# The row maxima of an attention stage turned by VectorE in 32x32 blocks instead of by TensorE, sent in 128-byte pieces, and SyncE's sends in another order

## Chip, core and metric

One core of a Trainium2 chip. The metric is the device time in microseconds of the whole program, as the median of its runs.

## What is computed

For an input x of 8 x 1024 x 256 the result is x + attention(LN(x)) + experts(LN(x)). The attention has 16 heads of 16 channels and an ALiBi bias:

```python
kqv = x @ W_kqv.T
k_, q_, v_ = jnp.split(kqv, 3, axis=-1)
...
bias = alibi_slopes(H)[:, None, None] * rel.astype(jnp.float32)
score = jnp.einsum('bhsd,bhnd->bhsn', q, k) / scale + bias[None]
attn = jax.nn.softmax(score, axis=-1)
out = jnp.einsum('bhsn,bhnd->bhsd', attn, v)
```

The other part is a mixture of 8 experts (top 2) with a shared expert, in its own stages of the kernel, which the change does not touch.

## The kernel before

The program has three stages: `front` (layer norm, projections, routing, shared expert), `experts`, and `attend`, which the change is in. `attend` works on 32 groups of 4 heads of one batch (GROUPS, GH). For each group keys, queries and values lie in one of three sets of buffers, `k_op`, `q_op` and `v_op`. A softmax needs the row maxima before the exponentials, so every score is made twice. The first time (L1405, `max_half`) it lies with queries on the partitions, in the two PSUM buffers `p1`, and VectorE reduces it to `part` (L1255, `max_unit`, 1024 columns at a time); after 8 such units `join` (L1263) puts the smaller of the two negated halves into 8 columns of `neg`. The second time (L1418, `score`) keys lie on the partitions, in the three PSUM buffers `p2`, and the negated maximum of each query comes in as row 50 (or 114 for the second head of a pair) of `q_op`, beside a row of ones in `k_op`. ScalarE takes the exponential into `probs` (L1379), and TensorE multiplies that with the values into `p_o` (L1430, `products`). Every half group of 512 queries is copied to `o_sb` (L1367, `output_copy`), turned (L1442) and copied to `o_t` (L1357).

The two are offset by a group: while the scores of group g are made, the maxima of group g + 1 are made beside them, a score on one half of the array's rows and a maxima matmul on the other. A group has 64 units n of scores (HALF = 32 of them per half) and 32 units w of maxima (MAX_UNITS). TensorE's loop over n writes score n, maxima half n, and after each odd n one side of the products of 4 units ago. It begins a PSUM buffer of `p2` when `s2_read` tells that ScalarE has read it, and one of `p1` when `s1_read` tells that VectorE's reduction of two units before is done.

To get from `neg` (queries on partitions) to a row of `q_op`, TensorE transposes the 16 columns of a half's `neg` (L1411, `turn_max`) into a `p2` buffer: for the second half of the own group at n = 5 (OWN_TURN), and for the first half of the next group at n = 37 (TURN_AT). ScalarE copies it to `m_row`, 16 rows of 128 (L1348, `row_copy`). SyncE (SP) then sends it with 4 DMAs (L1144, `send_max`), each of which writes 4 pieces of 512 B into one row of `q_op`. The scores of a half wait for these DMAs (`m_in`) at the half's first unit. `use2` counts the uses of `p2`, the turns among them.

SP's program in a group is written out in `group` under `block.sync`: first the wait for the products of the group before (`pv_done`) and the 15 DMAs that load group g + 2 (L171, L175, L177, `load`), then `send_max` of the own second half, then `send_max` of the next group's first half. SP issues in this order. VectorE's program in a group is 32 reductions, 4 joins (each one unit late, but the last one right after the last unit) and up to two reciprocals (L1271, `invert`). Before group 0 stands a prologue of 32 maxima units without scores.

Of the kernel before, what the change touches and what calls it, by code (L numbers as in the profile page):

```python
# [1055 lines left out]
def attend(nc, keep, scratch, out):  # L1056
    with ExitStack() as ctx:
# [9 lines left out]
        neg = [sb(f"neg{i}", [P, 8 * PAIRS], F32R) for i in range(2)]  # L1067
        m_row = [sb(f"m_row{i}", [8 * PAIRS, P], F32R) for i in range(2)]
# [13 lines left out]
        names = ("passed ones_in init s1_ps s1_read neg_ok s2_ps s2_read pv_done pv_side o_ok rec_ok "  # L1082
# [11 lines left out]
        TURN_AT = HALF + 5  # L1094
        OWN_TURN = 5
# [3 lines left out]
        K_LOAD = 14  # L1099

        def ring1(g):
            return (g + 1) * R1

        def turns_at(g):

            out = [OWN_TURN] + [h * HALF + OUT_TURN for h in range(2) if g or h]
            return sorted(out + ([TURN_AT] if g < GROUPS - 1 else []))

        def use2(g, n):

            before = 1 + sum(UNITS + len(turns_at(i)) for i in range(g))
            return before + n + sum(t < n for t in turns_at(g))
# [16 lines left out]
        def _(sp):  # L1129
# [20 lines left out]
            send_max(0, 0, 0, 0)  # L1150
# [94 lines left out]
        def _(dve):  # L1245
            v = nc.vector

            dve.sem_inc(s["s1_read"], 2)

# [8 lines left out]
            def join(c_, done):  # L1258
# [4 lines left out]
                v.tensor_tensor(neg[half][:, 8 * pair:8 * pair + 8], pt[:, 0].rearrange("p x q -> p (x q)"),  # L1263
                                pt[:, 1].rearrange("p x q -> p (x q)"), ALU.min).then_inc(s["neg_ok"], 1)
# [39 lines left out]
            for w in range(MAX_UNITS):  # L1304
                max_unit(w, w)
                if w % CHUNK == CHUNK - 1:
                    join(w // CHUNK, w + 3)

            def group(g, u, turn, has_prev, has_next):
                due = None  # L1310
                for w in range(MAX_UNITS):
                    if has_next:
                        max_unit(ring1(g) + w, w)
                        if due is not None:
                            join(*due)
                            due = None
                        if w % CHUNK == CHUNK - 1:
                            due = (w // CHUNK, ring1(g) + (w + 3))
                    for half in range(2):
# [17 lines left out]
        def _(act):  # L1337
# [31 lines left out]
            row_copy(0, 0, 0)  # L1369

            def group(g, u, turn, has_prev, has_next):
                for n in range(UNITS):
# [7 lines left out]
                    if n == OWN_TURN:  # L1380
                        row_copy(g, use + 1, 1)
                    elif n == TURN_AT and has_next:
                        row_copy(g + 1, use + 1, 0)
                    elif n % HALF == OUT_TURN and (half or has_prev):
# [10 lines left out]
        def _(pe):  # L1395
# [11 lines left out]

            def turn_max(g, half, use):
                pe.wait_ge(s["neg_ok"], g * CHUNKS + PAIRS * (half + 1))
# [125 lines left out]
```

## Time and profile before

| | |
|---|---|
| median of the runs | 2465.36 us (3 runs, 2455.23 to 2470.11) |
| span of the profiled execution | 2465.2 us |
| the profiled execution's own time | the page gives the span alone |
| TensorE (PE) busy | 2399.8 us, 97% |
| VectorE (DVE) busy | 1899.4 us, 77% |
| ScalarE (ACT) busy | 1561.3 us, 63% |
| GpSimd (POOL) busy | 782.9 us, 32% |
| mean granted TensorE clock | 0.982 of full speed |

PE is a TensorE matmul, PEld its weight load, SPq the issue of a DMA on SyncE's queue. Times in a timeline are microseconds from the span's start. "x8" behind a row means that eight instructions in a row were merged into it; the second number is the time from the start of the first to the end of the last, as they overlap. The number of a matmul's end is modelled. In square brackets stands the idle time before a row, and what ended it. L numbers are lines of the kernel before.

### The profile page before, as it was taken

What the parts mean: (1) busy time and instruction counts of PE and PEld (TensorE: products, weight loads), DVE (VectorE), ACT (ScalarE), POOL (GpSimd) and SP (SyncE); (2) the same over time, 40 slices, a digit from 0 to 9 for tenths busy, and PEclk for the clock granted to TensorE, in tenths of its full rate; (3) what the DMA queues carried; (4) which work ended last, traced back from release to release, by engine and by line L of the source; (5) the groups of instructions that cost most, each with busy time, mean ns of one, the idle gap of its engine ahead of it and who ended that gap; (6) DMA issues with size and microseconds to landing.
All of it is one profiled execution on the core that took longest, in us unless ns stands there. A gap on an engine that the chain in (4) does not pass through costs nothing.

```text
span 2465.2 us, 53774 instructions
## 1 busy us (share of the span) xinstructions
PE 2399.8 (97%) x19426; PEld 1490.7 (60%) x19426; DVE 1899.4 (77%) x2889; ACT 1561.3 (63%) x3276; POOL 782.9 (32%) x901
## 2 busy tenths in 40 slices
PE   8999999996999999989999999999999999999998
PEld 7888888886999999963333333333333333333333
DVE  6666566655556555568999999999999999999994
ACT  3333333333343333315888888888888888888888
POOL 2222323225242222210113333333333333333333
PEclk9999999997999999987999999999999999999999
DMA  6999877771332222232425343434344443435321
GB/s 189 185 166 176 172 129 148 140 120 35 87 98 76 76 75 76 77 74 47 84 49 103 62 88 71 87 72 84 74 79 80 74 85 72 87 67 91 64 58 40
DMA packets 177924, 229.05 MB, mean 93 GB/s; under 512 B 42828, under 2 KB 127436, under 8 KB 177656
## 3 DMA queue, kind: packets, MB, share of 16 engines
q1 hardware_dynamic: 153048, 172.02, 37.6%
q0 software_dynamic: 22448, 50.56, 8.6%
q8 instruction: 168, 2.75, 0.5%
q10 hardware_dynamic: 2176, 3.02, 0.3%
q14 instruction: 84, 0.69, 0.1%
HBM read 131.47 MB, written 93.66 MB: 91 GB/s over the span
## 4 chain that ended last, share of the span: by engine, by line
PE 52%; DVE 2%; DMA 1%; ACT 0%; issue 0%; SPq 0%; DVEq 0%; ACTq 0%
PE p_o L1430 23%; PE p L1418 18%; PE p L1405 9%; PE p L1442 1%; DVE part L1255 1%; DMA q_op<-m_row 1%; PE p L1411 1%; ACT probs L1379 0%; SPq L1144 0%; ACT o_sb L1367 0%; DVE neg L1263 0%; DVE att L1282 0%; DVE att L1302 0%; ACT o_t L1357 0%; DVE rec L1279 0%
## 5 line engine op out<-in xcount | busy, mean ns | idle before, releaser
L1255 DVE TENSOR_REDUCE part<-p 128x2 f32<-128x1024 f32 x1024 | 1237.8, 1221 | 79.9 <-PE p L1405 64.8
L1379 ACT ACTIVATE probs<-p 128x512 f32<-128x512 f32 x2048 | 1109.2, 596 | 159.6 <-PE p L1418 122.8
L1405 PE MATMUL p<-k_op,q_op 50*128 50x512 f32 x2048 | 757.2, 461 | 14.0 <-DVE part L1255 10.9
L1418 PE MATMUL p<-q_op,k_op 51*128 51x512 f32 x2048 | 756.5, 451 | 1.9 <-DMA q_op<-m_row 0.7
L1430 PE MATMUL p_o<-probs,v_op 128*32 128x256 f32 x8192 | 657.4, 392 | 5.1 <-ACT o_sb L1367 1.3
L1418 PEld LDWEIGHTS p<-q_op,k_op 51*128 51x128 f32 x2048 | 312.6, 186 | 417.3 <-ACT probs L1379 355.9
L1430 PEld LDWEIGHTS p_o<-probs,v_op 128*32 128x32 f32 x8192 | 163.3, 108 | 359.7 <-ACT probs L1379 285.0
L1405 PEld LDWEIGHTS p<-k_op,q_op 50*128 50x128 f32 x2048 | 307.0, 189 | 29.3 <-DVE part L1255 26.1
L1206 POOL TENSOR_TENSOR att<-o_t,rec 128x256 f32<-128x256 f32 x63 | 39.0, 618 | 809.1 <-DVE rec L1271 809.1
L828 POOL DMA_INDIRECT xe<-xn_scratch,ids x135 | 146.3, 1083 | 340.4 <-DMA ids<-lists_scratch 309.9
L921 ACT ACTIVATE gated_e<-p_gate 128x352 f32<-128x352 f32 x135 | 62.8, 465 | 194.9 <-PE p_gate L859 115.6
L941 DVE TENSOR_TENSOR xet_lo<-pe_x,xet_hi 128x256 fp32r<-128x256 f32 x135 | 57.3, 424 | 151.5 <-ACT xet_hi L911 145.9
L367 POOL DMA_INDIRECT lists_scratch<-token,slot_c x128 | 126.6, 989 | 77.5 <-issue 38.9
L602 ACT CAST h_hi<-h_sb 128x512 fp32r<-128x512 f32 x96 | 59.5, 620 | 141.6 <-DVE h_sb L432 130.6
L649 PE MATMUL p_u<-xt_hi,s_gu_hi 128*128 128x512 f32 x352 | 142.9, 406 | 6.3 <-DVE s_dn_lo L532 3.8
L649 PE MATMUL p_u<-xt_hi,s_gu_lo 128*128 128x512 f32 x352 | 139.7, 397 | 0.0
L649 PE MATMUL p_u<-xt_lo,s_gu_hi 128*128 128x512 f32 x352 | 139.7, 397 | 0.0
L878 PE MATMUL pe_y<-wdn_hi,ht_hi 128*128 (+1 forms) x405 | 125.5, 310 | 1.8 <-DVE ht_lo L1011 1.8
L931 ACT CAST ht_hi<-pe_h 128x256 fp32r<-128x256 f32 x135 | 50.4, 373 | 120.2 <-PE pe_h L868 114.9
L356 POOL TENSOR_TENSOR root<-ve,half 128x4 f32<-128x4 f32 x16 | 21.8, 1364 | 325.4 <-DVE ve L386 325.4
L1216 POOL DMA_INDIRECT y_c<-yr_scratch,yslot_i x112 | 112.3, 1003 | 35.4 <-issue 35.4
L878 PE MATMUL pe_y<-wdn_hi,ht_lo 128*128 (+1 forms) x405 | 113.9, 281 | 0.0
(186 smaller groups left out, 4052.7 us busy)
## 6 DMA issues: line engine op xcount, KB each, us to landing
k_op<-qk_scratch SPq DMA_DIRECT2D x192, 128.0 KB
q_op<-qk_scratch SPq DMA_DIRECT2D x192, 128.0 KB
yr_scratch<-x SPq DMA_DIRECT2D x135, 128.0 KB
qk_scratch<-k_op SPq DMA_DIRECT2D x32, 512.0 KB
qk_scratch<-q_op SPq DMA_DIRECT2D x32, 512.0 KB
v_scratch<-v_op SPq DMA_DIRECT2D x16, 1024.0 KB
v_op<-v_scratch SPq DMA_DIRECT2D x32, 512.0 KB
x<-in_x SPq DMA_DIRECT2D x16, 512.0 KB
```

What stands on the lines that cost most here:

```text
L367: g.indirect_dma_start(scratch["lists"], bass.IndirectOffsetOnAxis(slot_c[n % 2][:, k, b:b + 1], 0), token[:, n * TB + b:n * TB + b + 1], ...
L602: a.copy(h_hi[j % HR][rows], h_sb[j % 2][rows]).then_inc(s["h_hi_ok"], 1)
L649: last = t.matmul(dst, lhs[a](k), rhs[b](k), start=(n == 0), stop=(n == 3 * KD - 1))
L828: g.indirect_dma_start(x_sb[u][:], None, scratch["xn"], bass.IndirectOffsetOnAxis(ids[u][:], 0)).then_inc(rt[f"x_in{u}"], 16)
L878: last = t.matmul(p_y[:, 0:D], ht[a][par][0:rows, c], dn[b][0:rows, ds(off + c * D, D)], start=(i == 0 and sub == 0), stop=(i == all_ - 1 ...
L921: a.activation(gated[u % 2][:], p_gate[:, 0:F], ACT.Silu).then_inc(q["gated"], 1)
L1216: g_.indirect_dma_start(y_c[k][u][:], None, scratch["yr"], bass.IndirectOffsetOnAxis(slot_i[:, k, n:n + 1], 0)).then_inc(s[f"yg_in{u}"], 16)
L1255: v.tensor_reduce(part[c_ % 2][:, kh, :, qb], p1[use % 2][:], AX.X, ALU.max, negate=True).then_inc(s["s1_read"], 1)
L1379: a.activation(probs[kb % 4][:, h], p2[use % 3][:], ACT.Exp).then_inc(s["s2_read"], 1)
L1405: return t.matmul(p1[use % 2][:, x], q_op[u][lo:lo + S1_ROWS, pair, q0:q0 + P], k_op[u][lo:lo + S1_ROWS, pair, kh * 512:(kh + 1) * 512], s ...
L1418: t.matmul(p2[use % 3][:], k_op[u][lo:lo + S2_ROWS, pair, kb * P:(kb + 1) * P], q_op[u][lo:lo + S2_ROWS, pair, half * HQ:(half + 1) * HQ], ...
L1430: ins = t.matmul(p_o[32 * h:32 * h + 32, cols], v_op[u][:, kb, VW * h:VW * h + VW], probs[kb % 4][:, h, cols], start=(kb == 0 and side == ...
```

## The change

The turn moves from TensorE and ScalarE to VectorE. `neg` gets 32 columns per half, of which 16 to 31 are set to zero once, and `join` writes its 8 values in another order of columns (head of the pair, then pair, then 4 blocks of queries). `turn_max` is now an instruction of VectorE, which turns the four 32x32 blocks of `neg` on its own (L1270 in the kernel after) into `m_t`: row 32b + j holds column j for queries 32b to 32b + 31. The piece that belongs to a row of `q_op` thereby comes in parts of 32 numbers, 128 B, and `send_max` has 8 DMAs (2 pairs, 4 blocks b), each of which writes two rows of `q_op` in 4 pieces. VectorE turns the second half of the own group after unit w = 1 and the first half of the next group after w = 17 (TURN_AFTER). TensorE and ScalarE have no turns of maxima any more, so the numbering of `p2` changes. On SP `send_max` of the own second half now stands ahead of the loads of group g + 2, and so ahead of the wait for `pv_done`.

```diff
-        neg = [sb(f"neg{i}", [P, 8 * PAIRS], F32R) for i in range(2)]
-        m_row = [sb(f"m_row{i}", [8 * PAIRS, P], F32R) for i in range(2)]
+        neg = [sb(f"neg{i}", [P, 32]) for i in range(2)]
+        m_t = [sb(f"m_t{i}", [P, 32]) for i in range(2)]
...
-        TURN_AT = HALF + 5
-        OWN_TURN = 5
+        TURN_AFTER = (MAX_UNITS // 2 + 1, 1)
...
+        M_LOAD = 8 * 16
...
 def turns_at(g):
-            out = [OWN_TURN] + [h * HALF + OUT_TURN for h in range(2) if g or h]
-            return sorted(out + ([TURN_AT] if g < GROUPS - 1 else []))
+            return [h * HALF + OUT_TURN for h in range(2) if g or h]
...
-            def send_max(g, u, half, use):
-                sp.wait_ge(s["s2_read"], use + 4)
+            def send_max(g, u, half):
+                sp.wait_ge(s["m_t_ok"], 2 * g + half + 1)
                 for pair in range(PAIRS):
-                    for x in range(2):
-                        r = 64 * x + S2_ROWS - 1
-                        sp.dma_start(q_op[u][r:r + 1, pair, half * HQ:(half + 1) * HQ]
-                                     .rearrange("o (q c) -> o q c", q=4).bitcast(F32),
-                                     m_row[half][8 * pair + 4 * x:8 * pair + 4 * x + 4].bitcast(F32)).then_inc(m_in[half], 16)
+                    for b in range(4):
+                        j = 32 * b + 8 * pair
+                        sp.dma_start(q_op[u][S2_ROWS - 1:S2_ROWS + 64:64, pair, half * HQ:(half + 1) * HQ]
+                                     .rearrange("x (q b c) -> x q b c", q=4, b=4)[:, :, b].bitcast(F32),
+                                     m_t[half][j:j + 8]).then_inc(m_in[half], 16)
...
             def group(g, u, turn, has_prev, has_next):
-                if has_next and not (isinstance(g, int) and g + 2 >= GROUPS):
+                send_max(g, u, 1)
+                if has_next and g + 2 < GROUPS:
                     if has_prev:
                         sp.wait_ge(s["pv_done"], g * (2 * NK) + NK)
                     else:
                         sp.wait_ge(s["init"], NB_OP - 1)
-                    load((g + 2) % GROUPS, (u + 2) % 3)
-                send_max(g, u, 1, use2(g, OWN_TURN) + 1)
+                    load(g + 2, (u + 2) % 3)
                 if has_next:
-                    send_max(g + 1, following(u, turn)[0], 0, use2(g, TURN_AT) + 1)
+                    send_max(g + 1, following(u, turn)[0], 0)
...
             dve.sem_inc(s["s1_read"], 2)
+            for half in range(2):
+                v.memset(neg[half][:, 16:32], 0.0).then_inc(s["neg_set"], 1)
+            dve.wait_ge(s["neg_set"], 2)
...
-                v.tensor_tensor(neg[half][:, 8 * pair:8 * pair + 8], pt[:, 0].rearrange("p x q -> p (x q)"),
-                                pt[:, 1].rearrange("p x q -> p (x q)"), ALU.min).then_inc(s["neg_ok"], 1)
+                mine = neg[half][:, 0:16].rearrange("p (j x q) -> p j x q", x=2, j=PAIRS)[:, pair]
+                v.tensor_tensor(mine, pt[:, 0], pt[:, 1], ALU.min).then_inc(s["neg_ok"], 1)
+
+            def turn_max(g, half):
+                dve.wait_ge(s["neg_ok"], g * CHUNKS + PAIRS * (half + 1))
+                if g:
+                    dve.wait_ge(m_in[half], g * M_LOAD)
+                v.transpose(m_t[half][:], neg[half][:]).then_inc(s["m_t_ok"], 1)
...
+                        if w == TURN_AFTER[0]:
+                            turn_max(g + 1, 0)
                         if w % CHUNK == CHUNK - 1:
                             due = (w // CHUNK, ring1(g) + (w + 3))
+                    if w == TURN_AFTER[1]:
+                        turn_max(g, 1)
...
-            def row_copy(g, use, half):
-                act.wait_ge(s["s2_ps"], use + 1)
-                if g:
-                    act.wait_ge(m_in[half], g * (32 * PAIRS))
-                a.copy(m_row[half][:], p2[use % 3][0:8 * PAIRS, 0:P]).then_inc(s["s2_read"], 1)
...
-            def turn_max(g, half, use):
-                pe.wait_ge(s["neg_ok"], g * CHUNKS + PAIRS * (half + 1))
-                pe.wait_ge(s["s2_read"], use + 1)
-                t.transpose(p2[use % 3][0:8 * PAIRS, 0:P], neg[half][:].bitcast(F32), ident[:]).then_inc(s["s2_ps"], 1)
```

VectorE's program around the first turn of a group, as the chip gets it; `part` is the result of a reduction, `p_0` and `p_1` the two buffers of `p1`. Before, from the last reciprocal of a group on:

```order
L1271 RECIPROCAL rec<-o_t 128x16
L1255 TENSOR_REDUCE part<-p_0 128x2
L1255 TENSOR_REDUCE part<-p_1 128x2
L1255 TENSOR_REDUCE part<-p_0 128x2
L1255 TENSOR_REDUCE part<-p_1 128x2
L1263 TENSOR_TENSOR neg<-part 128x8
L1255 TENSOR_REDUCE part<-p_0 128x2
L1255 TENSOR_REDUCE part<-p_1 128x2
L1255 TENSOR_REDUCE part<-p_0 128x2
```

And now, at the same place:

```order
L1277 RECIPROCAL rec<-o_t 128x16
L1255 TENSOR_REDUCE part<-p_0 128x2
L1255 TENSOR_REDUCE part<-p_1 128x2
L1255 TENSOR_REDUCE part<-p_0 128x2
L1255 TENSOR_REDUCE part<-p_1 128x2
L1264 TENSOR_TENSOR neg<-part 128x8
L1255 TENSOR_REDUCE part<-p_0 128x2
L1255 TENSOR_REDUCE part<-p_1 128x2
L1270 STREAM_TRANSPOSE m_t<-neg 128x32
L1255 TENSOR_REDUCE part<-p_0 128x2
```

One instruction was added, between the group's second and third reduction.

TensorE's program at a turn before, with `p_0` to `p_2` the buffers that a matmul writes:

```order
L1418 MATMUL p_1<-q_op,k_op 128x512
L1405 MATMUL p_0<-k_op,q_op 128x512
L1418 MATMUL p_2<-q_op,k_op 128x512
L1405 MATMUL p_0<-k_op,q_op 128x512
L1411 MATMUL p_0<-ident,neg 16x128
L1430 MATMUL p_o<-probs,v_op 32x256 x4
L1418 MATMUL p_1<-q_op,k_op 128x512
```

And now, at such a place:

```order
L1412 MATMUL p_1<-q_op,k_op 128x512
L1404 MATMUL p_1<-k_op,q_op 128x512
L1412 MATMUL p_2<-q_op,k_op 128x512
L1404 MATMUL p_1<-k_op,q_op 128x512
L1424 MATMUL p_o<-probs,v_op 32x256 x4
L1412 MATMUL p_0<-q_op,k_op 128x512
```

The products follow straight on the scores, and the next score takes the buffer of `p2` that the turn had.

SP's queue of a steady group before. A row's shape is what one DMA writes, and x8 are the sends of both halves, which stand one behind the other:

```order
L171 DMA k_op<-qk_scratch 16x2x1024 x6
L171 DMA q_op<-qk_scratch 16x2x1024 x6
L175 DMA k_op<-ali_scratch 2x2x1024 x2
L177 DMA v_op<-v_scratch 128x8x128
L1144 DMA q_op<-m_row 1x4x128 x8
```

And now, where the 16 are the first-half send of one group and the second-half send of the next turn of the loop, each with its wait for `m_t_ok`, and the first load waits for `pv_done`:

```order
L1143 DMA q_op<-m_t 2x4x32 x16
L171 DMA k_op<-qk_scratch 16x2x1024 x6
L171 DMA q_op<-qk_scratch 16x2x1024 x6
L175 DMA k_op<-ali_scratch 2x2x1024 x2
L177 DMA v_op<-v_scratch 128x8x128
```

The second-half send went from behind the loads to ahead of them, and each send has twice the DMAs.

## Rows read from the trace of the kernel before

**Rows 1.** The page: busy time by engine, share of the span, instructions.

```profile
PE 2399.8 (97%) x19426; PEld 1490.7 (60%) x19426; DVE 1899.4 (77%) x2889; ACT 1561.3 (63%) x3276; POOL 782.9 (32%) x901
```

**Rows 2.** Busy time by stretch: length, PE, PEld, DVE, ACT, POOL, clock, DMA share, GB/s.

```profile
1089.00:1125.00 36.00, 24.70 (x65) 8.72 (x61) 35.73 (x35) 1.54 (x2) 7.64 (x6) 0.50 0.81 134
1125.00:1143.00 18.00, 17.60 (x93) 6.17 (x93) 11.63 (x11) 9.89 (x19) 0.00 (x0) 0.50 0.17 31
...
1505.00:1546.00 41.00, 40.90 (x394) 15.72 (x386) 38.76 (x38) 36.13 (x73) 15.46 (x20) 1.00 0.43 79
...
2419.00:2438.00 19.00, 18.66 (x169) 7.32 (x165) 1.42 (x3) 17.47 (x36) 11.23 (x15) 1.00 0.16 47
```

**Rows 3.** Waits in 1143:2460: who waited for whom, us in total, times, longest.

```profile
PEld p L1418 <- ACT probs L1379: 351.0, 888, 0.8
...
DVE part L1255 <- PE p L1405: 56.2, 120, 0.9
...
PEld p L1411 <- issue: 22.8, 62, 0.4
...
PEld p L1418 <- DMA q_op<-m_row: 3.9, 7, 0.9
```

**Rows 4.** Timeline of PE around a turn: start us, us, instruction.

```profile
1504.63 0.64 PE L1430 MATMUL p_o<-probs,v_op 128*32 128x256 f32 x8
...
1505.87 0.64 PE L1430 MATMUL p_o<-probs,v_op 128*32 128x256 f32 x8
...
1507.23 0.64 PE L1430 MATMUL p_o<-probs,v_op 128*32 128x256 f32 x8
...
1508.46 0.28 PE L1411 MATMUL p<-ident,neg 128*16 128x128 f32 x1
1508.67 0.64 PE L1430 MATMUL p_o<-probs,v_op 128*32 128x256 f32 x8
...
1509.90 0.64 PE L1430 MATMUL p_o<-probs,v_op 128*32 128x256 f32 x8
...
1510.47 0.73 PE L1405 MATMUL p<-k_op,q_op 50*128 50x512 f32 x2
```

**Rows 5.** The tile m_row: durations in ns (least, median, most), and who waited.

```profile
L1144 SPq DMA_DIRECT2D q_op<-m_row x256: 572/573/647, 1110.4 to 2425.2; - x128
L1348 ACT CAST m_row<-p x64: 238/238/255, 1110.1 to 2423.1; 16x128 fp32r<-16x128 f32 x64
...
  PE p L1418: 0.7, 3
```

**Rows 6.** Timeline of DVE in the same group.

```profile
1506.03 0.39 DVE L1263 TENSOR_TENSOR neg<-part 128x8 fp32r<-128x8 f32 x1
1506.34 3.49 DVE L1255 TENSOR_REDUCE part<-p 128x2 f32<-128x1024 f32 x3
...
1517.96 0.15 DVE L1263 TENSOR_TENSOR neg<-part 128x8 fp32r<-128x8 f32 x1
1518.06 3.71 DVE L1255 TENSOR_REDUCE part<-p 128x2 f32<-128x1024 f32 x3
1521.68 0.24 DVE L1271 RECIPROCAL rec<-o_t 128x16 f32<-128x16 f32 x1
1521.84 6.12 DVE L1255 TENSOR_REDUCE part<-p 128x2 f32<-128x1024 f32 x5
```

**Rows 7.** Timeline of SP's queue in the same group.

```profile
1507.92 2.64 SPq L171 DMA_DIRECT2D k_op<-qk_scratch  x6
...
1514.91 16.58 SPq L1144 DMA_DIRECT2D q_op<-m_row  x6
...
1530.30 1.80 SPq L1144 DMA_DIRECT2D q_op<-m_row  x3
```

**Rows 8.** Chain that ended last, in order of time: from issue to landing.

```profile
2180.79 9.77 DMA q_op<-m_row
```

**Rows 9.** Busy time by stretch of 5 us in that group; columns as in rows 2.

```profile
1510.00:1515.00 5.00, 5.00 (x50) 2.07 (x52) 4.74 (x4) 4.24 (x9) 0.54 (x1) 1.00 0.99 161
...
1525.00:1530.00 5.00, 4.95 (x51) 1.67 (x47) 4.84 (x6) 4.69 (x11) 4.20 (x6) 1.00 0.19 56
```

More of the change, by code:

```diff
@@ L1080, in attend @@
         p_o = ps("p_o", [P, HQ])
-        names = ("passed ones_in init s1_ps s1_read neg_ok s2_ps s2_read pv_done pv_side o_ok rec_ok "
+        names = ("passed ones_in init neg_set m_t_ok s1_ps s1_read neg_ok s2_ps s2_read pv_done pv_side o_ok rec_ok "
                  "pool_c o_st0 o_st1 att_ok o_out base_in0 base_in1 yg_in0 yg_in1 fin_base fin_y "
@@ L1104, in turns_at @@
         def turns_at(g):
-            out = [OWN_TURN] + [h * HALF + OUT_TURN for h in range(2) if g or h]
-            return sorted(out + ([TURN_AT] if g < GROUPS - 1 else []))
+            return [h * HALF + OUT_TURN for h in range(2) if g or h]
         def use2(g, n):
-            before = 1 + sum(UNITS + len(turns_at(i)) for i in range(g))
+            before = sum(UNITS + len(turns_at(i)) for i in range(g))
             return before + n + sum(t < n for t in turns_at(g))
@@ L1137, in load @@
                     load_operand(sp, keep, scratch, k_op[u], q_op[u], v_op[u], g, u, i)
-            def send_max(g, u, half, use):
-                sp.wait_ge(s["s2_read"], use + 4)
+            def send_max(g, u, half):
+                sp.wait_ge(s["m_t_ok"], 2 * g + half + 1)
                 for pair in range(PAIRS):
-                    for x in range(2):
-                        r = 64 * x + S2_ROWS - 1
-                        sp.dma_start(q_op[u][r:r + 1, pair, half * HQ:(half + 1) * HQ]
-                                     .rearrange("o (q c) -> o q c", q=4).bitcast(F32),
-                                     m_row[half][8 * pair + 4 * x:8 * pair + 4 * x + 4].bitcast(F32)).then_inc(m_in[half], 16)
+                    for b in range(4):
[3 more added lines that the diff above has]
+                                     m_t[half][j:j + 8]).then_inc(m_in[half], 16)
             sp.wait_ge(s["init"], 1)
             load(1, 1)
-            send_max(0, 0, 0, 0)
+            send_max(0, 0, 0)
             def group(g, u, turn, has_prev, has_next):
-                if has_next and not (isinstance(g, int) and g + 2 >= GROUPS):
+                send_max(g, u, 1)
+                if has_next and g + 2 < GROUPS:
                     if has_prev:
@@ L1307, in _ @@
                     join(w // CHUNK, w + 3)
+                if w == TURN_AFTER[0]:
+                    turn_max(0, 0)
             def group(g, u, turn, has_prev, has_next):
@@ L1316, in group @@
                             due = None
+                        if w == TURN_AFTER[0]:
+                            turn_max(g + 1, 0)
                         if w % CHUNK == CHUNK - 1:
                             due = (w // CHUNK, ring1(g) + (w + 3))
+                    if w == TURN_AFTER[1]:
+                        turn_max(g, 1)
                     for half in range(2):
@@ L1379, in group @@
                     a.activation(probs[kb % 4][:, h], p2[use % 3][:], ACT.Exp).then_inc(s["s2_read"], 1)
[L1380 to L1384, printed above, removed]
+                    if n % HALF == OUT_TURN and (half or has_prev):
                         turned_copy(*((g, 0) if half else (g - 1, 1)), use + 1)
@@ L1450, in _ @@
                 max_half(0, w, w, 0).then_inc(s["s1_ps"], 1)
-                if w == MAX_UNITS // 2 + 2:
-                    turn_max(0, 0, 0)
             def group(g, u, turn, has_prev, has_next):
@@ L1463, in group @@
                     if l == 0:
-                        pe.wait_ge(m_in[half], (g + 1) * (32 * PAIRS))
+                        pe.wait_ge(m_in[half], (g + 1) * M_LOAD)
                     if n == 0:
```

5 lines of the change are left out of this document (removed).

## Prediction

> **What bounds the kernel now.** I read the page first. TensorE (PE) is busy 97% of the span [rows 1]. The change touches only the attention stage, which begins at about 1088 us, so the second view is the table of stretches [rows 2]. It shows three regimes. In 1089:1125, where only the maxima of group 0 are made, DVE is busy 35.73 of 36 us and sets the pace, at a granted clock of 0.50. In a steady group (1505:1546) PE is busy 40.90 of 41 us, DVE 38.76 and ACT 36.13: PE sets the pace, but DVE is close behind; the granted clock is 1.00 there. In the last group (2419:2438) no maxima are made; DVE has 1.42 us of work and ACT 17.47 of 19.
>
> The third view is the waits [rows 3]. From 1143 us on DVE waits 56.2 us for PE in 120 places. The list has no wait of the maxima matmuls for DVE. PE's waits for the maxima's DMA are small: 3.9 us in 7 places, and 0.7 us in 3 [rows 5]. So in some 30 groups nearly every us taken from PE shortens the time, as long as DVE's slack is not used up first.
>
> **What a turn costs PE.** PE works in a fixed beat: eight products (L1430), then two scores and two maxima matmuls side by side. The start of the products marks it [rows 4]: 1504.63, 1505.87, 1507.23, 1508.67, 1509.90. The plain beats are 1.24 and 1.23 us, of which I take 1.24. The beat that holds the transposition of the maxima (L1411, at 1508.46) is 1.44 us, so a turn costs 1.44 - 1.24 = 0.20 us, less than its own 0.28 us since it overlaps the products. The beat before it is 1.36 us; its extra 0.12 us is a wait for ACT's copy of the output, which the change leaves. The waits list counts 62 turns in the steady part (L1411, 62 times) [rows 3]. Removed: 62 x 0.20 = 12.4 us. The two others of the 64 lie in the prologue, under DVE's work, and in the last group, where ACT sets the pace: without the copy to m_row (0.24 us, [rows 5]) I credit 0.2 us there. ACT's other 63 copies lie in ACT's waits and give nothing more.
>
> **What the turn costs DVE.** Three kinds of work are added: 64 transpositions of 128x32, two memsets and a differently strided output of the join. The memsets come after DVE has released PE, while PE makes the first maxima: nothing. The strided join writes the same 8 elements: nothing. The trace has no DVE transposition. What matters is c, how much later the next reduction starts. In a catching-up row three reductions take 3.49 us, one of them 1.22 long, so they start (3.49 - 1.22) / 2 = 1.13 us apart [rows 6], against PE's beat of 1.24. A reciprocal on 16 elements pushes the next reduction by 1521.84 - 1521.68 = 0.16 us; a join without a drain by 1518.06 - 1517.96 = 0.10. Those are the near rows; the far end is the reduction itself, 1.22 us. I take c = 0.16, between 0.10 and 1.22.
>
> The Trainium skill, "VectorE: DVE Perf Modes", section "The three transpose paths", gives 311 ns for VectorE on 128x128 bf16 and says that it only turns 32x32 blocks. No row here shows it; with c = 0.31 the sum below would be the same, as that too is under the limit that follows.
>
> Is c hidden? After the group's first join the reductions start at 1506.34, 1507.47 and 1508.61. The transposition goes ahead of the third, which then ends at 1509.83 + c. It reads the PSUM buffer that PE writes again at 1510.47 (L1405) [rows 4], or 0.20 earlier without the turn: 1510.27. That leaves 0.44 us, about 0.4 for a semaphore's way. In the second half the join costs 0.10 instead of the 0.31 of the first (1506.03 to 1506.34), so the limit is about 0.6. With c = 0.16 nothing reaches PE. In the DVE-bound prologue one transposition is uncovered: +0.2 us.
>
> **What the reordering on SP gives and costs.** Now SP issues 15 loads from 1507.92, and the second-half maxima only at 1514.91 [rows 7]. They are queued behind the loads. The chain shows one that took 9.77 us from the last issue to landing, with PE late behind it [rows 8]. Of the 3.9 us in 7 waits, some 0.40 each is the pause that every score has (351.0 / 888) [rows 3]. So 3.9 - 2.8 + 0.7 = 1.8 us is lost; I credit 1.8, between 0 and 4.6. Afterwards these pieces leave at about 1508.8, 16 us before they are needed, with nothing in front.
>
> The price is on SP. A send has 8 DMAs instead of 4. One issue takes 0.573 us [rows 5]; with the gap after it 0.61 to 0.62 (three took 1.80 us, [rows 7]), so the send takes 8 x 0.62 = 5.0 us. The loads then start at 1513.8 instead of 1507.9, 5.9 us later. The DMA engines are full at 1510:1515 (0.99), and down to 0.19 at 1525:1530 [rows 9]: the loads land at about 1525, then about 1531. They are needed at the next group's start, some 15 us later. The first-half send for the next group becomes ready at about 1529.3 (before: 1530.30), is issued until 1534.3, and is needed at 1546.2: 12 us, against the 9.8 that this landing behind loads took. Both are hidden.
>
> The Trainium skill bears on this, in "DMA: Bandwidth & Descriptors". Its "Specifications" ask for 512 B for line rate and have smaller writes done as read-modify-write, and "Why a DMA increments its semaphore by 16 and not by 1" has a copy split over the largest number of engines that divides both slowest dimensions: 2 for the new shape (2x4x32 from 8 rows), 4 for the old one (1x4x128 from 4). By it the new pieces land later than the old. No row shows it. It would not enter the sum unless it cost over 12 us, and it is why the third rival has a chance at all.
>
> **Sum.** The execution's span is 2465.2 us; the page gives no time around it, and the median of the runs, 2465.36, is the same within 0.2. 2465.2 - 12.4 (turns) - 1.8 (late maxima) - 0.2 (last group) + 0.2 (prologue) = 2451.0, and +0.2 for the median: 2451.2. From 1088 to 1143 us PE runs at 0.50 of its clock [rows 2]. If that stretch ends 5 us earlier or later, about 2.5 us come or go; this and the scatter of the three runs (2455 to 2470) widen the likeliest one's own range to 2443 to 2459.
>
> **Rivals.** (1) More gain: the 0.12 us pause of the beat ahead of the turn goes too (less work on ACT), 62 x 0.32 = 19.8, and all 4.6 us of the waits are real: 24.4 off, 2441. For it: ACT loses 15 us of work. Against it: the pause comes from ACT's output copy, which stands ahead of the copy to m_row in ACT's program.
> (2) DVE takes PE's place, in the second to fourth beat after each turn. From c = 0.4 in first and 0.6 in second halves PE waits for the reduction. Break-even: 31(c - 0.4) + 31(c - 0.6) = 14.2, c = 0.73. At c = 1.22, as long as a reduction of 1024 columns, 31 x 0.82 + 31 x 0.62 = 44.6 us are lost: 2465 - 14 + 45 = 2496. For it: DVE is 94% busy. Against it: a turn has 32 columns, and every short DVE row pushes by under 0.2.
> (3) The first-half maxima come late, since 64 pieces of 128 B on few engines stand behind loads that are 5.9 us later. It decides from a landing 12 us after the last issue; at 13 us PE waits 1 us in each of 31 groups: 2451 + 31 = 2482. Against it: the old one took 9.8 with all the loads right in front of it.
> (4) The turn's gap doesn't close, as DVE, with 56 us of idle over 31 groups, or ACT takes it up: only the 1.8 us, 2463. Against it: DVE's reductions can follow 1.13 us apart [rows 6], and its 120 waits for PE are some four in each group [rows 3].
>
> **Chances.** Forecast 0.74, (1) 0.08, (2) 0.06, (3) 0.03, (4) 0.09. One per cent, 24.7 us, is about what a measurement of this kernel tells from no change. The forecast and (4) lie within it, (1) at its edge: faster by over 1% 0.05, within 0.87, slower 0.08. The range takes in (1) and (4) and the scatter of a median: 2440 to 2465.
>
> **What would show it.** Right: no L1411 and no m_row; all beats 1.23 to 1.24 us but those with output copies and output turns; 41.1 us from one group to the next, 0.4 less than now; the second-half maxima with more than 10 us to spare and no wait for them in the list; reductions that start under 0.25 us later after a transposition. Wrong: waits of L1405's successor for the reduction two beats after a turn (rival 2), scores waiting at a group's start for the maxima's DMA (rival 3), beats of 1.44 us that stay (rival 4).

## The result and the profile after

The changed kernel takes 2472.8 us (median of 20 runs, 2461.62 to 2487.68), the kernel before 2464.61 (20 runs, 2455.23 to 2473.73). The ratio is 1.0037, with a 95% interval of 1.0023 to 1.0051: slower by 0.4%, where the prediction had 0.6% faster and a range that ended at 2465. Groups and halves below are those of one profiled execution of each kernel.

The page of the changed kernel, span and busy times, against [rows 1]:

```profile
span 2470.1 us, 53841 instructions
PE 2397.9 (97%) x19362; PEld 1484.6 (60%) x19362; DVE 1905.6 (77%) x2955; ACT 1548.7 (63%) x3212; POOL 782.7 (32%) x901
```

PE has 64 matmuls fewer, ACT 64 instructions fewer and 12.6 us less work, DVE 66 instructions more. The work went where the change sends it, and the span grew by 4.9 us all the same. (The medians lie 8.2 us apart. A run's time is 1.8 us over its span wherever both are on record, so the profiled execution of the kernel before took about 2467 us, 2.4 over its median, and that of the changed kernel 2471.93, 0.9 under its own.) To find where, I took the start of the first score matmul of each half group from the two timelines (2048 scores, 32 in a half) and subtracted them:

```
stretch (us)                        before     after
start to the first score            1125.1    1122.4
group 0                               47.5      46.8
groups 1 to 30 (60 halves)          1246.4    1253.8
group 31 and the end                  46.3      47.1
halves 2 to 7, about                 20.73     20.56
first halves from group 10 on        20.73     21.03   (medians)
second halves from group 10 on       20.77     20.83   (medians)
```

Before the first score the two executions differ by 2.7 us in stages that the change doesn't touch. In groups 1 to 3, before POOL's first gather of expert rows, the changed kernel has the gain that was forecast, 0.17 us in most halves. From group 4 on it loses it and more: the 30 groups cost 7.4 us more than before, though 60 x 0.17 = 10 us were to be gained.

Here is PE's timeline in the first half of group 10, which begins at 1543.71. The products' starts mark the beats, as in [rows 4]:

```profile
1545.74 0.64 PE L1424 MATMUL p_o<-probs,v_op 128*32 128x256 f32 x8
...
1547.00 0.64 PE L1424 MATMUL p_o<-probs,v_op 128*32 128x256 f32 x8
...
1548.24 0.64 PE L1424 MATMUL p_o<-probs,v_op 128*32 128x256 f32 x8
1548.81 0.50 PE L1412 MATMUL p<-q_op,k_op 51*128 51x512 f32 x1
...
1549.15 0.40 PE L1412 MATMUL p<-q_op,k_op 51*128 51x512 f32 x1
1549.48 0.64 PE L1424 MATMUL p_o<-probs,v_op 128*32 128x256 f32 x8
1550.05 0.50 PE L1412 MATMUL p<-q_op,k_op 51*128 51x512 f32 x1
...
1550.82 0.50 PE L1412 MATMUL p<-q_op,k_op 51*128 51x512 f32 x1 [0.27 <-ACT probs L1382]
...
1551.25 0.64 PE L1424 MATMUL p_o<-probs,v_op 128*32 128x256 f32 x8
```

The beat that held the turn is 1547.00 - 1545.74 = 1.26 us, where it was 1.44. Two beats of 1.24 follow. Then comes one of 1551.25 - 1549.48 = 1.77: the second score starts 0.77 us after the first instead of 0.34, since ACT has not freed its buffer. ACT, DVE, SP and POOL show why, in the same stretch:

```profile
1548.10 1.08 ACT L1382 ACTIVATE probs<-p 128x512 f32<-128x512 f32 x2 [0.17 <-PE p L1412]
1550.17 2.06 ACT L1382 ACTIVATE probs<-p 128x512 f32<-128x512 f32 x4 [0.98 <-PE p L1412]
...
1547.17 0.20 DVE L1270 STREAM_TRANSPOSE m_t<-neg 128x32 f32<-128x32 f32 x1
1547.29 2.32 DVE L1255 TENSOR_REDUCE part<-p 128x2 f32<-128x1024 f32 x2
1550.25 2.37 DVE L1255 TENSOR_REDUCE part<-p 128x2 f32<-128x1024 f32 x2 [0.63 <-PE p L1404]
...
1547.39 4.26 SPq L1143 DMA_DIRECT2D q_op<-m_t  x8
1551.70 0.40 SPq L171 DMA_DIRECT2D k_op<-qk_scratch  x1
...
1546.79 1.03 POOL L1213 DMA_INDIRECT y_c<-yr_scratch,yslot_i  x1 [0.30 <-issue]
1548.12 0.99 POOL L1213 DMA_INDIRECT y_c<-yr_scratch,yslot_i  x1 [0.30 <-issue]
```

PE issued scores 8 and 9 of the half at 1548.81 and 1549.15, and their modelled ends are 1549.31 and 1549.55. But ACT stands idle for 0.98 us and takes score 8 at 1550.17 only, then four scores back to back; and DVE, which waits for PE's maxima and not for a score, stands idle for 0.63 us and goes on at 1550.25. Two engines that wait for different matmuls are released together, while PE's issue had gone on in its beat (1549.48, 1550.05). So it is PE's completions, or their signals, that came late, by some 0.8 us (ends are modelled, so the trace can't tell the one from the other). It comes at score 8 in each half from group 5 to the first one of group 31, with one exception, and that is the stretch in which POOL issues two gathers of expert rows (3.0 and 4.4 us into a half) and SP a send (from 3.7 us on in first halves, 3.4 in second ones). The exception and the second half of group 4 say the same: there the two gathers stand at 5.4 and 6.7 us of the half, and the late scores are 11 to 13, by up to 1.9 us, while the kernel before has none late by over 0.6 us in these two halves. What is late moves with the gathers.

The kernel before has it too, but less. In the second half of group 9 (start 1525.93), where SP's send (4 DMAs) began at 4.4 us, as the second gather did:

```profile
1530.51 1.09 ACT L1379 ACTIVATE probs<-p 128x512 f32<-128x512 f32 x2 [0.24 <-issue]
1532.08 3.27 ACT L1379 ACTIVATE probs<-p 128x512 f32<-128x512 f32 x6 [0.48 <-PE p L1418]
```

ACT stands idle for 0.48 us there. In the first half of group 10, where only loads of SP's lie under the gathers, it is 0.25:

```profile
1552.49 2.22 ACT L1379 ACTIVATE probs<-p 128x512 f32<-128x512 f32 x4 [0.25 <-PE p L1418]
```

PE has buffers enough to lose nearly nothing by either.

The waits of the changed kernel in 1140:2460, against [rows 3]:

```profile
ACT probs L1382 <- PE p L1412: 107.9, 433, 1.2
...
DVE part L1255 <- PE p L1404: 66.3, 124, 1.9
...
PE p L1412 <- ACT probs L1382: 4.3, 16, 0.7
```

There is no wait for the maxima's DMA any more; those late maxima are gone. The list names ACT only for 4.3 us of the time that PE's scores waited, because a late buffer stretches the matmuls beside it, and a row of the weight load (349.9 us) mixes it with ordinary pauses. The starts of the beats showed the loss, the waits didn't.

### The profile page after: what moved, and what is told of

Its sections match the earlier page's. It is cut to its first block, busy times and chain, and to the rows that moved or that the text cites. A ratio compares the mean times of both kernels' runs of the same rounds, so it can differ in the third digit from the quotient of the medians.

```text
span 2470.1 us, 53841 instructions
## 1 busy us (share of the span) xinstructions
PE 2397.9 (97%) x19362; PEld 1484.6 (60%) x19362; DVE 1905.6 (77%) x2955; ACT 1548.7 (63%) x3212; POOL 782.7 (32%) x901
## 4 chain that ended last, share of the span: by engine, by line
PE 53%; DVE 2%; ACT 1%; issue 0%; DVEq 0%
PE p_o L1424 23%; PE p L1412 20%; PE p L1404 9%; DVE part L1255 2%; PE p L1436 2%; ACT probs L1382 1%; ACT o_sb L1372 0%; DVE neg L1264 0%; DVE att L1288 0%; DVE att L1308 0%; DVE rec L1285 0%; DVE m_t L1270 0%; DVEq L1245 0%; DVEq L1254 0%
## 5 line engine op out<-in xcount | busy, mean ns | idle before, releaser
L1404 PE MATMUL p<-k_op,q_op 50*128 50x512 f32 x2048 | 767.7, 462 | 14.4 <-DVE part L1255 11.4
L1412 PE MATMUL p<-q_op,k_op 51*128 51x512 f32 x2048 | 766.9, 452 | 8.2 <-ACT probs L1382 4.6
```

Of the source, the lines that this page charges most:

```text
L1404: return t.matmul(p1[use % 2][:, x], q_op[u][lo:lo + S1_ROWS, pair, q0:q0 + P], k_op[u][lo:lo + S1_ROWS, pair, kh * 512:(kh + 1) * 512], s ...
L1412: t.matmul(p2[use % 3][:], k_op[u][lo:lo + S2_ROWS, pair, kb * P:(kb + 1) * P], q_op[u][lo:lo + S2_ROWS, pair, half * HQ:(half + 1) * HQ], ...
```

## The experiments

Three theories stood. A: SP's send, running while POOL gathers, holds up PE's completions. B: the gathers alone do, and the shorter beat of PE moved a score under them. C: SP's send alone does. All kernels below start from the changed one, where not said otherwise. "Gap" is ACT's idle time before score 8 in the first half of group 10 (0.15 us in an ordinary beat), and halves are medians from group 10 on. Lines of a kernel shift with its edits: L1374 and L1394 are the exponential too.

**Turns and sends later.**

```diff
-        TURN_AFTER = (MAX_UNITS // 2 + 1, 1)
+        TURN_AFTER = (MAX_UNITS // 2 + 4, 4)
```

> The changed kernel with VectorE's turns three units later (after w = 4 and w = 20), so that SP's 8 issues of a send start about 7.4 us into a half instead of 3.7. Theory A (the loss is SP's sends running while GpSimd's second gather of a half is under way, 4.4 to 6.4 us into the half): nothing of SP's stands in that window, the late score 8 of each half goes, halves of 20.56 us from group 5 on as in groups 1 to 3 of the changed kernel, time about 17 us below the changed kernel, near 2453. Theory B (the gathers alone hold TensorE's completions up, and the beat moved under them when the turn left TensorE): the halves stay at 21.03 and 20.75 on average, time as the changed kernel, 2470.

Measured: 2453.64 us, ratio to the kernel before 0.9953 (0.9916 to 0.999). Both kinds of halves are 20.55 us, and groups 1 to 30 take 1233.5 us, 20.3 less than in the changed kernel. ACT, SP and POOL in the first half of group 10 (start 1532.43):

```profile
1538.24 2.15 ACT L1382 ACTIVATE probs<-p 128x512 f32<-128x512 f32 x4 [0.32 <-PE p L1412]
...
1539.72 2.11 SPq L1143 DMA_DIRECT2D q_op<-m_t  x4
...
1536.79 0.99 POOL L1213 DMA_INDIRECT y_c<-yr_scratch,yslot_i  x1 [0.30 <-issue]
```

The gather stands where it stood, 4.36 us into the half, the send starts at 7.3, and the gap is 0.32 instead of 0.98. PE's beat is the short one here too: B falls as the cause of the loss.

It holds for a smaller part. From the second gather's issue to ACT's start on score 8 pass 1.45 us here and 1.51 in the first halves of the kernel before (medians from group 10 on), though score 8 comes about 0.2 us earlier in the half now. So with nothing of SP's near, ACT gets score 8 some 0.2 us after its modelled end, where 0.04 is ordinary. That costs PE nothing. In the second halves of before, with a send beside the gather, 1.79 us pass, and in the first halves of the changed kernel 2.05.

**SP's old order.**

```diff
-                send_max(g, u, 1)
                 if has_next and g + 2 < GROUPS:
...
                     load(g + 2, (u + 2) % 3)
+                send_max(g, u, 1)
```

> The changed kernel with SP's old order: loads of group g + 2 ahead of the send of the own second half. Theory A: in first halves the loads' issues lie over the gather in place of a send, and first halves come down from 21.03 to 20.6 to 20.7 us; second halves stay near 20.75 or worse, as the second-half send now comes late or the first-half send is unchanged; time about 12 us below the changed kernel, with some late second-half maxima. Theory B: both kinds of halves as in the changed kernel, 2470.

Measured: 2471.19 us, ratio 1.0042 (1.0014 to 1.0069), where the changed kernel has 1.0037: the 12 us that were expected off are not there; first halves 20.75, second halves 20.81, but groups 1 to 30 take 1263.0 us, with single halves of 22 to 26 us. Its waits in 1160:2400:

```profile
PEld p L1412 <- DMA q_op<-m_t: 17.7, 20, 2.0
PE p L1412 <- DMA q_op<-m_t: 8.4, 14, 1.5
```

The loads lie over the gather in first halves, with a gap of 0.38 us, as theory A had it; in second halves, where the send is ahead of the gather still, it stays at 0.69 (median). What was gained goes to second-half maxima that come late: with 8 DMAs behind the loads there are 34 waits for them, where the kernel before had 10. Two of the long halves, of over 26 us, also hold the only stretches between 1150 and 2470 us in which the granted clock was 0.50 (10 us from 1323 on and 14 us from 1781 on). So with 8 DMAs the send is better ahead of the loads.

**No gathers.** This run leaves out `y_c`'s gathers and its terms in `combine`, and so a part of the result.

```diff
-                for k in range(2):
-                    g_.indirect_dma_start(y_c[k][u][:], None, scratch["yr"],
-                                          bass.IndirectOffsetOnAxis(slot_i[:, k, n:n + 1], 0)).then_inc(s[f"yg_in{u}"], 16)
...
-                for k in range(2):
-                    y = y_c[k][u]
-                    c.link(g_.tensor_scalar(y[:], y[:], wts[:, k, n:n + 1], None, ALU.mult))
-                    c.link(g_.tensor_tensor(acc[:], acc[:], y[:], ALU.add))
```

> The changed kernel without GpSimd's gathers of expert rows (y_c) for batches 0 to 6 and without their terms in the output: it leaves out the experts' part of the result there. Both theories: the late score 8 goes and all halves are 20.56 us, 18 us below the changed kernel, 2452 or a little less. If the halves stay at 21.03 and 20.75, GpSimd has no part in it, and theory C is next: SP's 8 sends alone hold TensorE's completions up.

Measured: 2444.66 us, ratio 0.9934 (0.9905 to 0.9964), 7 us below what was expected, which its groups don't explain (groups 1 to 30 take 1234.0 us, as with the later turns); all halves 20.56 us, though SP's send stands at 3.4 us as in the changed kernel. ACT around score 8:

```profile
1538.75 1.09 ACT L1374 ACTIVATE probs<-p 128x512 f32<-128x512 f32 x2 [0.15 <-PE p L1404]
```

A gap of 0.15 us is the ordinary pause: C falls. Gathers and send must come together. (POOL's arithmetic on the gathered rows is gone too; the last run below clears it.)

**The order alone, in the kernel before.** `send_max` of the own second half ahead of the loads, with TensorE's turn and 4 DMAs.

> The kernel before with SP's new order alone: the send of the own second half (4 DMAs of 512-byte pieces, TensorE's turn) ahead of the loads. Theory A: in first halves a send now lies over the gather (issued from 4.4 us on), score 8 comes late by 0.3 to 0.4 us as it does in second halves, which the slack takes up, so halves stay near 20.73 and the late maxima go: 1 to 2 us faster than before. Theory B: the same, as order doesn't matter; 1 to 2 us faster. If first halves grow by 0.2 us or more, the order of SP alone costs what the change lost.

Measured: 2460.11 us, ratio 0.999 (0.9972 to 1.0009); halves 20.77 and 20.79, groups 1 to 30 1246.0 us (before: 1246.4). Its halves grow by 0.02 to 0.04, about what the late maxima may have given. The order of SP is not what cost the time, and no gain by it alone can be told from none.

**Number of DMAs, or their start.** There are two runs: the turns one unit later, and half of the send left out, so that half of the maxima are old ones.

```diff
-        TURN_AFTER = (MAX_UNITS // 2 + 1, 1)
+        TURN_AFTER = (MAX_UNITS // 2 + 2, 2)
```

> The changed kernel with VectorE's turns one unit later (after w = 2 and w = 18), so that SP's issues of a send start at about 4.9 us into a half, near the 5.1 of TensorE's turn in the kernel before, with 8 DMAs instead of 4. Theory N (how many small DMAs SP issues before and in the window of GpSimd's second gather counts): score 8 is late by 0.6 to 0.8 us as in the changed kernel, halves stay at 20.8 to 21.0. Theory S (how early the send starts counts, since then its DMAs are in flight when the gather comes): score 8 is late by some 0.37 us as in the kernel before, halves 20.55 to 20.6.

```diff
-                    for b in range(4):
+                    for b in range(2):
...
-        M_LOAD = 8 * 16
+        M_LOAD = 4 * 16
```

> The changed kernel with 4 of the 8 DMAs of each send (blocks b = 0 and 1 only): it leaves out the maxima of half of the queries, whose row then holds older numbers. Start and shape are those of the changed kernel, SP's issues end at 5.8 us into the half instead of 8. Theory N: the late score 8 comes down to 0.4 us or less and halves to 20.6. Theory S: it stays at 0.6 to 0.8 us and halves at 20.8 to 21.0.

Measured, later start: 2455.7 us, ratio 0.9963 (0.9914 to 1.0012), halves 20.55. Measured, half of the send: 2472.34 us in one run, halves 21.03 and 20.84, the changed kernel's to 0.01 us. ACT, SP and POOL in the first half of group 10, first of the later start (half from 1547.39), then of the half send (from 1545.32):

```profile
1553.28 2.07 ACT L1382 ACTIVATE probs<-p 128x512 f32<-128x512 f32 x4 [0.40 <-PE p L1412]
...
1552.17 4.26 SPq L1143 DMA_DIRECT2D q_op<-m_t  x8
...
1551.75 0.99 POOL L1213 DMA_INDIRECT y_c<-yr_scratch,yslot_i  x1 [0.30 <-issue]
```

```profile
1551.74 2.07 ACT L1382 ACTIVATE probs<-p 128x512 f32<-128x512 f32 x4 [0.94 <-PE p L1412]
...
1548.96 2.11 SPq L1143 DMA_DIRECT2D q_op<-m_t  x4
...
1549.69 0.98 POOL L1213 DMA_INDIRECT y_c<-yr_scratch,yslot_i  x1 [0.30 <-issue]
```

Theory N falls for these halves and S stands. A send that starts 0.4 us after the second gather's issue (1552.17 against 1551.75) costs a gap of 0.40, whole as it is; one that starts 0.7 us ahead of it (1548.96 against 1549.69) costs 0.94, even with half of its DMAs. It is not the doubled count of DMAs, but that the send moved from the gather's start, or behind it, to ahead of it. (In the last group the count does show; see there.)

**What the DMAs move.** The kernel with the later turns, and 8 spare DMAs of the old shape between two tiles of their own, where the changed kernel has its send:

```diff
+            def spare(units, done):
+                sp.wait_ge(s["s1_read"], 2 + units)
+                sp.wait_ge(s["d_in"], 16 * 8 * done)
+                for i in range(8):
+                    sp.dma_start(d_dst[:, i], d_src[:]).then_inc(s["d_in"], 16)
```

> The kernel with the turns three units later, halves of 20.55 us, and with 8 spare DMAs issued by SP from 3.7 us into each half on, when the changed kernel's send would start; each moves 4 pieces of 512 B between two tiles that nothing else uses. It adds work and changes no result. If issues of small DMAs by SP hold TensorE's completions up under the gather whatever they move: halves of 20.8 to 21.0, as in the changed kernel. If it is the 128-byte pieces, or writes to q_op while TensorE reads it: halves stay under 20.65.

Measured: 2452.12 us in one run; first halves 20.71, second 20.55, groups 1 to 30 1237.9 us; gap 0.60. This lies between the two answers: 8 DMAs that touch nothing of the kernel's, ahead of the gather, bring 0.16 us in first halves, 4.4 us on the whole. The rest of the loss must hang on the pieces' shape or their target.

**Spare DMAs in the kernel before.** TensorE's turns and its own sends stay; 4 DMAs of the new shape are added from 3.5 us into each half on.

> The kernel before with TensorE's turns and all its own sends, and 4 spare DMAs added in each half, of the new shape (8 rows of 32 numbers into two rows, 128-byte pieces) but between two tiles that nothing else uses; SP issues them from about 3.7 us into a half on. It adds work and changes no result. If DMAs of this shape that start ahead of the second gather are enough: score 8 comes late by 0.6 to 0.8 us here too and halves grow from 20.73 to 20.9 to 21.1, 10 to 20 us on the whole. If it needs the write into q_op, or the beat without TensorE's turn: halves stay under 20.8.

Measured: 2528.05 us in one run, far over what was expected; first halves 21.55, second 20.93. ACT, SP and POOL in a first half (from 1585.66), then its waits in 1160:2400:

```profile
1592.09 2.07 ACT L1394 ACTIVATE probs<-p 128x512 f32<-128x512 f32 x4 [0.77 <-PE p L1433]
...
1589.22 2.21 SPq L1153 DMA_DIRECT2D d_dst<-d_src  x4
...
1590.06 0.98 POOL L1230 DMA_INDIRECT y_c<-yr_scratch,yslot_i  x1 [0.30 <-issue]
```

```profile
PEld p L1433 <- DMA q_op<-m_row: 36.4, 27, 2.9
PE p L1433 <- DMA q_op<-m_row: 23.4, 21, 2.4
```

The gap of 0.77 us came into the kernel before with the spare DMAs, and the beat from score 10 to score 12 grew from 1.25 to 1.47 us (medians of first halves): they are enough, without a write to `q_op` and without the change. Most of its 63 us is another thing: the spares push the loads back by 3 us and the own second half's send, behind them, from 9.3 to 12.4 us into the half, and PE waits 59.8 us in 48 places for maxima. The granted clock also fell to 0.50 seven times between 1237 and 1784 us, for 68 us in all. So this run shows the gap, and not what the gap costs.

**Transposition or send.** VectorE's turns where the change has them, SP's send held until unit w = 3 (w = 19) is reduced.

```diff
+                if has_next:
+                    sp.wait_ge(s["s1_read"], 2 + ring1(g) + 4)
                 send_max(g, u, 1)
...
                 if has_next:
+                    sp.wait_ge(s["s1_read"], 2 + ring1(g) + MAX_UNITS // 2 + 4)
                     send_max(g + 1, following(u, turn)[0], 0)
```

> The changed kernel with VectorE's turns where they are (after w = 1 and w = 17), but SP holds each send until the reduction of w = 3 or w = 19 is done, about 6 us into the half. If the send that is under way when GpSimd's second gather is issued (4.4 us) causes the late score 8: halves of 20.55 us, 2453. If VectorE's transposition at 3.5 us is the cause (its work just ahead of score 8): halves stay at 21.03 and 20.83, 2470.

Measured: halves 20.55 and 20.55, groups 1 to 30 1234.1 us, gap 0.38. So it is the send, not VectorE's turn, which stands where the change has it. But the whole took 2468.88 us, ratio 1.0021 (0.9998 to 1.0043), not 2453: its profiled execution lost some 12 us in the last group, told of below.

**One gather.** This has `for k in range(1)` in `fetch` and `combine`, and leaves out the second expert's term.

> The changed kernel with one gather of expert rows per half instead of two; it leaves out the second expert's term for batches 0 to 6. If the second gather's issue at 4.4 us under SP's send is what holds score 8 up: score 8 on time, halves 20.56. If the first gather (3.0 us) with its data at 4.8 to 5.3 us does it: the halves stay at 20.8 to 21.0.

Measured: 2449.93 us in one run, halves 20.56, no gap. It doesn't say which of the gathers matters: with less to combine, the one that is left moved from 3.0 to 1.1 us into the half, far ahead of the send.

**The later turns again**, for an interval:

> The kernel of e1_turn_later again, word for word, for an interval of its own: 0.995 of the kernel before (0.992 to 0.998), halves of 20.55 us.

Measured: 2453.53 us, ratio 0.9954 (0.9935 to 0.9973), halves 20.55.

**Gathers away from the send.** The turns and sends of the change stay; POOL fetches ahead of combining:

```diff
+                if NK - 2 <= x_no < first + NK - 2:
+                    fetch(x_no - (NK - 2))
                 if x_no >= NK - 1:
                     pool.wait_ge(s["att_ok"], x_no + 1)
                     combine(x_no - (NK - 1))
-                if NK - 2 <= x_no < first + NK - 2:
-                    fetch(x_no - (NK - 2))
```

> The changed kernel, its turns and sends where they are, with GpSimd's order in a half swapped: it fetches the next block's rows (one load, two gathers) ahead of combining this block, so the gathers are issued at about 16 to 18 us into the half before, when SP issues nothing, and not at 3.0 and 4.4 us. If the loss needs gathers and SP's send together, whichever of the two is moved: score 8 on time and halves of 20.55 to 20.6 us in both halves, 2453, 0.995 of the kernel before. If a gather delays whatever completes some 1.3 us after it wherever it stands: the late score moves to the end of the half and halves stay above 20.8.

Measured: 2450.11 us, ratio 0.9937 (0.9912 to 0.9961), all halves 20.56, groups 1 to 30 1235.3 us. ACT around score 8 and SP's send in the first half of group 10 (from 1541.49):

```profile
1547.12 1.09 ACT L1382 ACTIVATE probs<-p 128x512 f32<-128x512 f32 x2 [0.15 <-PE p L1412]
...
1545.13 4.26 SPq L1143 DMA_DIRECT2D q_op<-m_t  x8
```

The send is the change's, at 3.6 us, and the gap is gone; the gathers now stand at 18.1 and 19.4 us of the half, and POOL's arithmetic on the rows where they stood. The loss goes whichever of the two is moved. A gather still delays what completes soon after it (DVE starts the second reduction of a second half 0.44 us after its matmuls' end instead of 0.07), but that is taken up by slack. This has the lowest median of the kernels here that compute everything, 0.6% under the kernel before; its interval overlaps that of the later turns (0.9935 to 0.9973).

## Why the prediction was wrong

**What a turn costs PE: right.** 0.20 us a turn was forecast and the beat went from 1.44 to 1.26, that is 0.18. A half without the late score takes 20.56 instead of 20.73 us. With the sends out of the gathers' way, a group takes the 41.1 us that were forecast, and groups 1 to 30 take 1233.5 us instead of 1246.4: 12.9 us off, where 62 x 0.20 + 1.8 = 14.2 stood in the sum for 31 groups.

**What the turn costs DVE: right.** c was taken as 0.16 us; the reduction after a transposition starts 1547.29 - 1547.17 = 0.12 us after it. The tile's row gives a duration of 200 ns. Nothing of it reached PE: with the turns in place and only the send held, halves took 20.55 us. Rival 2 had the sign of the result by another way: DVE never took PE's place.

**What the reordering gives: the waits went, the 1.8 us are not shown.** The waits for the maxima's DMA are gone from the list, and the order alone made no difference that could be measured (2460.11 against 2460.27 us).

**What the reordering and the send cost on SP: here it failed.** The step said of the pieces that they leave at 1508.8 "with nothing in front", and of their price "Both are hidden". It priced a send by when its pieces land and by what it pushes back, and there it held: a send of 8 took 4.26 us where I had 5.0, no maxima came late, and rival 3 didn't happen. It never asked what the send does to others while it runs. Started 0.7 us ahead of POOL's second gather instead of with it or behind it, it made PE's completions late once in a half, by 0.82 us in first halves and 0.62 in second ones (medians, from a score's modelled end to ACT's start). About 0.34 us of a lateness are taken up: 0.82 cost 0.48 us of a half, 0.62 cost 0.28, and the 0.50 of the spare DMAs cost 0.16. Over 30 groups that is 1253.8 - 1233.5 = 20.3 us, a term that the sum had at nothing. 12.9 gained less 20.3 lost are the 7.4 us that these groups take longer than before. The trace of before held the warning in the two rows of ACT shown above: 0.48 us idle at score 8 with a send beside the gather, 0.25 without one. I had read PE's row, which lost nothing by it.

**When the pieces land.** No row here gives the landing of a send, only that no score waited for one in the changed kernel. The prediction weighed the Trainium skill's page "DMA: Bandwidth & Descriptors", sections "Specifications" and "Why a DMA increments its semaphore by 16 and not by 1", by which it had the new pieces land later; nothing here contradicts it or bears it out, and it wasn't what decided. For the turn itself the Trainium skill's page "VectorE: DVE Perf Modes", section "The three transpose paths", gives 311 ns for a 128x128 bf16 transposition; here one of 128x32 in float took 200 ns.

**The last group.** 0.2 us less were forecast for the copy that ACT no longer makes; its first half went from 19.14 to 19.91 us. It has the late scores too, and more so: no maxima are made there, so the turn and its send come early, at 1.5 us, and the gathers stand at 3.0 and 4.4 us as ever. Score 8 is late by 1.26 us. It is late by 1.19 to 1.51 in every profiled kernel with such a send of 8 DMAs and both gathers in these places, the later turns among them, and by 0.88 where the send has 4. In the kernel before, whose send starts at 4.4 us, it is not late, nor is it in the kernels without the gathers or with moved ones, where the half takes 19.0 to 19.1 us.

## What to carry to other kernels

A DMA that is off the critical path is not free of cost for engines that never wait for it: here a send of 8 KB, in 8 DMAs, stretched TensorE's beat because it ran into another queue's gather. When a change moves transfers in time, look at what other queues do in the new place, and at the small idle times (0.2 to 0.5 us) of the engines with slack: they show how much of it is used already. And where an engine is busy 97% before and after, measure its beat from start to start in several places of the loop: neither busy time nor the list of waits showed this loss.

## What the runs showed of the hardware

PE's completions, as ACT and DVE see them, can come late by 0.8 us, and up to 1.9 us in single places, with PE's issue going on in time, when POOL issues gathers and SP small DMAs close together. The gap at score 8 was 0.15 us without gathers, and 0.32 to 0.40 with gathers and a send that starts after the second one or not at all in that stretch. It was 0.48 to 0.50 (medians) with 4 DMAs of 512-byte pieces that start with the second gather, 0.60 with 8 of them ahead of it, and 0.74 to 0.98 with 4 to 8 DMAs of 128-byte pieces ahead of it. Why is open: whether the matmuls' writes or their signals are held, and by which part of the two queues' work, no run here tells. Nor is the first gather told from the second, or the shape of the pieces from the number of rows that they come from.

The second finding is TensorE's clock in the last group. There PE has no maxima to make and waits for ACT. These are the kernel with later turns, in its first profile, then the kernel with the gathers moved, in the last group's first half:

```profile
2403.00:2430.00 27.00, 27.00 (x155) 8.00 (x154) 0.25 (x1) 17.38 (x34) 7.89 (x10) 0.50 0.07 20
```

```profile
2407.00:2425.00 18.00, 17.47 (x156) 6.78 (x155) 0.41 (x2) 16.47 (x34) 11.27 (x15) 1.00 0.11 31
```

In the first the last group begins at 2395.3 us at a granted clock of 1.00. Its score 8 is late, ACT stands idle for 1.27 us, and PE for 0.81; right after, at 2402.9, the granted clock is 0.50 (the lower of the two levels, 1.2 GHz):

```profile
2401.42 0.49 PE L1412 MATMUL p<-q_op,k_op 51*128 51x512 f32 x1
2402.71 0.63 PE L1412 MATMUL p<-q_op,k_op 51*128 51x512 f32 x1 [0.81 <-ACT probs L1382]
...
2402.06 2.06 ACT L1382 ACTIVATE probs<-p 128x512 f32<-128x512 f32 x4 [1.27 <-PE p L1412]
```

That half took 27.35 us instead of 19 to 20. The kernel with the held send shows the same order: PE idle for 0.91 us until 2417.08, 0.50 from 2418.4 on. In the changed kernel's profile PE was idle for 0.67 us at that place, and the clock stayed at 1.00.

The mean clocks of the runs go with it. Of the 51 runs of kernels with late scores in the last group but none of the long waits for maxima, 15 have a mean clock of 0.977 or less: 4 of 20 of the changed kernel, 3 of 6 and 1 of 7 of the later turns, 6 of 8 with the held send, 1 of 8 of the turns one unit later, and neither of the single runs of half the send and of the spare DMAs. Of the kernels without them (the kernel before in 60 runs, its new order alone, no gathers, one gather, moved gathers) none of 82 is under 0.979. So the late scores of the last group are the likely cause of these falls; no run moves them alone. The first runs of the later turns show what a fall costs: 2458 to 2468 us at a mean clock of 0.975 or less, 2445 to 2449 for the others. It is also the likely reason why the held send brought nothing on the whole. It explains little of the changed kernel's median, which without its four runs would be 2472.4 us.
